# The last stage of a graph network on one core: dinv in all partitions, scaling and transform on GpSimd, ReLU in the residual

## The chip, the cores and the metric

One core of one Trainium2 chip. The metric is the time of one execution on the device, in microseconds (us). The kernel before ran three times: 7513.93 us median, 7498.69 to 7516.11.

## The reference

12500 nodes with 128 features and 412500 edges. Two message-passing layers, each followed by a residual and a layernorm:

```
x = layernorm(x + L0(x))          # filter network on edges, scatter-add, two dense layers
x = layernorm(x + L1(x))

L1: xw = x @ W ;  dinv = rsqrt(degree)
    out = segment_sum(xw[src] * dinv[src] * dinv[dst], dst) + b
    out = (out - mean_over_nodes) * rsqrt(var_over_nodes + 1e-5) * gamma + beta
    return relu(out)
```

The change touches only what comes after the sums of L1: the factor dinv[dst], the batch norm over the nodes, the ReLU, the second residual and the last layernorm.

## The kernel before, in words

`program` runs five parts one after the other, each a block of its own with a program for each engine: `setup`, `filter_layer`, `node_update`, `graph_layer`, `norm_and_store`. The last one is the stage in question. When it begins, `arena` holds the sums of L1 with the 128 features in the partitions and the 12500 nodes along the columns; `x1_tab` in DRAM holds x after the first layernorm; `dinv_tab` in DRAM holds dinv. Nodes are dealt as 125 partitions (NP) times 100 (NC): node p * 100 + c. A batch q is 500 columns (BW); there are 25 batches (NB), each of B = 4 groups of 125 nodes.

Half A runs over the 25 batches. SP loads 500 values of dinv (2 KB) into one partition (L2676); PE multiplies them with a row of ones, so that PSUM holds them in all 128 partitions (L2694, two passes of a float32 matmul for a batch, so 50 in all); DVE multiplies the batch of `arena` in place by that PSUM tile (L2739) and takes its mean and variance with bn_stats (L2742). Two dinv rows and two PSUM tiles are in flight, and the counters `spread` and `scaled` hand them round. Meanwhile ACT's queue has issued five loads of x1 into `xs_flat`, 125 partitions each (L2710). After the last batch, DVE aggregates (L2745) and works out a scale and a shift for each feature in short instructions (L2747 to L2760), with one Sqrt on ACT (L2713).

Half B runs over the 25 batches again, as software pipelines on four engines. ACT waits for `bn_ready`, loads the table with Ln and Exp (L2716), and then in each round:

- transforms a batch: Relu(scale * x + shift), 128x500 (L2722). It reads `rows`, a view of `arena` whose inner step is 100 columns, so 400 bytes, and writes `turned`, dense;
- normalizes the rows of the batch before: four activations of 125x128 (`norm_rows_on_act`, L1842), into one of two `xn` buffers;
- takes the root of the variances as exp(-0.5 * ln(v)) (`norm_root`, L1817 and L1819, 125x4).

PE turns the transformed batch back with four transposes (L2702). DVE adds the PSUM tile to x1 (L2770), takes bn_stats of four rows (`norm_measure`, L1801), aggregates them (L1808), adds the epsilon (L1811, 125x4), and from ACT's root forms the shift of the rows (`norm_shift`, L1834, 125x4). SP stores each batch with one DMA of 125 rows of 2 KB (L2682).

The same helpers run in `node_update`, the part that makes x1. There GpSimd (POOL) is at work too: L1932, L1942 and L1945 are its tensor_tensor instructions of 125x512, and L2134 is a DVE tensor_tensor of 128x500 with both inputs in SBUF. In `setup`, POOL has L462 (affine_select) and L488 (tensor_tensor of 125x256). In `norm_and_store` POOL does nothing before the change.

Of the kernel before, what the change touches and what calls it, by code (L numbers as in the profile page):

```python
# [35 lines left out]
P = 128  # L36
# [13 lines left out]
B = 4  # L50
# [37 lines left out]
WIDE = 112  # L88
X_USED = 5858
MROW = 3 * F + 2  # L90
# [10 lines left out]
def free(g):  # L101
    return g + 1
# [1674 lines left out]
class Norm:  # L1777


    def __init__(self, m, at, sem):  # L1780
# [6 lines left out]
        self.shift = [m.work[0:NP, at + B * (12 + s):at + B * (13 + s)] for s in range(2)]  # L1787
        self.steps, self.waited, self.rooted, self.normed = sem("ln_steps"), sem("ln_waited"), sem("ln_rooted"), sem("ln_normed")
        self.shifted = sem("ln_shifted")
# [32 lines left out]
def norm_rows(nc, dve, m, norm, q, s, out):  # L1822
# [5 lines left out]
    last.then_inc(norm.normed, 1)  # L1828


def norm_shift(nc, dve, norm, q, s):

    dve.wait_ge(norm.rooted, 2 * q + 2)
    nc.vector.scalar_tensor_tensor(norm.shift[s], norm.pair[s][:, :, 0], -1.0, norm.rstd[s], ALU.mult,  # L1834
                                   ALU.mult).then_inc(norm.shifted, 1)


def norm_rows_on_act(nc, act, m, norm, q, s, out):

    act.wait_ge(norm.shifted, q + 1)  # L1840
    for t in range(B):
        last = nc.scalar.activation(out[:, D * t:D * t + D], xs_row(m, q, t), ACT.Identity,  # L1842
                                    bias=norm.shift[s][:, t:t + 1], scale=norm.rstd[s][:, t:t + 1])
    last.then_inc(norm.normed, 1)
# [801 lines left out]
def norm_and_store(nc, m, io):  # L2646

    ps, work = m.ps, m.work
    drow = [work[0:1, 512 * s:512 * s + BW] for s in range(2)]
# [4 lines left out]
    turned = [work[:, 1536 + 512 * s:1536 + 512 * s + BW] for s in range(2)]  # L2654
    xn = [work[0:NP, 2700 + 512 * s:3212 + 512 * s] for s in range(2)]
    ps_d = [ps[:, s, 0:BW] for s in range(2)]
    ps_r = [ps[0:NP, 2 + s, :] for s in range(2)]
    rows = m.arena[:, 0:N].rearrange("f (p c) -> f c p", c=NC)
    with ExitStack() as ctx:
        def sem(name):  # L2660
            return ctx.enter_context(nc.semaphore(name))
        row_in = [sem("dinv_row0"), sem("dinv_row1")]
        spread, scaled, bn_steps, bn_agg = sem("dinv_spread"), sem("sums_scaled"), sem("bn_steps"), sem("bn_aggregated")
        bn_std, bn_ready = sem("bn_std"), sem("bn_ready")
        relu_done, turned_back, res_done = sem("relu_done"), sem("turned_back"), sem("residual2")
        norm = Norm(m, 2600, sem)
        waited = sem("ln2_waited")
        stored = [sem("out_stored0"), sem("out_stored1")]
        x1_in = sem("x1_in")
        block = ctx.enter_context(nc.Block())  # L2670

        @block.sync
        def _(sp):
            def load(q, s, turn):
                sp.wait_ge(spread, free(q))
                sp.dma_start(drow[s], m.dinv_tab[bass.ds(q * BW, BW)].rearrange("(o n) -> o n", o=1)).then_inc(row_in[s], 16)  # L2676
            over(sp, NB, load)
            flat = io["out"].rearrange("(p c) d -> p (c d)", p=NP)

            def store(q, s, turn):  # L2680
                sp.wait_ge(norm.normed, ready(q, 2))
                sp.dma_start(flat[:, bass.ds(q * (B * D), B * D)], xn[s]).then_inc(stored[s], 16)  # L2682
            over(sp, NB, store)
            sp.wait_ge(stored[0], 16 * (NB // 2 + 2))
            sp.wait_ge(stored[1], 16 * (NB // 2 + 1))

        @block.tensor
        def _(pe):
            pe.sem_inc(spread, 2)
# [6 lines left out]
            pe.sem_inc(turned_back, 2)  # L2696

            def back(q, s, turn):
                pe.wait_ge(relu_done, ready(q, 0))
                pe.wait_ge(res_done, free(q))  # L2700
                for t in range(B):
# [105 lines left out]
```

## Time and profile before

| | |
|---|---|
| median of three runs | 7513.93 us |
| profiled execution, its time | 7511.49 us |
| its span, first to last instruction | 7509.8 us |
| mean granted TensorE clock | 0.763 |
| `norm_and_store` in the span | 7339.87 to 7509.8 us |
| half A, first load to the end of the last L2742 | 7339.87 to 7413.39 us |
| half B, from `bn_ready` | 7415.53 to 7509.8 us |

A span is cut into windows to see which engine is busy in which stretch; a row of the timeline is one instruction, or several of a line that follow each other (x4), with its start, its duration, its engine (PE and PEld are TensorE's matmuls and weight loads, DVE is VectorE, ACT is ScalarE, POOL is GpSimd, SP is SyncE), its line, what it writes and reads, and in brackets how long the engine stood idle before it and which instruction ended that. A granted clock of 0.50 is the 1.2 GHz level of TensorE, 1.00 the 2.4 GHz level.

### The profile page before, as it was taken

Reading aid. Unit: us, or ns where it says so; the run is one execution under the profiler, and the core shown is the slowest. Engines: PE = TensorE matmul, PEld = TensorE weight load, DVE = VectorE, ACT = ScalarE, POOL = GpSimd, SP = SyncE. Lnnn points to the kernel's source line nnn. Section 1 sums busy time; section 2 is a strip of 40 time slices with the busy share of each in tenths; the row PEclk is TensorE's granted clock in tenths of the full one; section 3 lists DMA queues with packets and bytes.
Section 4 is the critical chain, followed back from the end, with each engine's and each line's share of the span. In section 5 each row is a group of like instructions: output and inputs, shape, how many; then the busy total and the mean of one; then the engine's idle time right before and its main releaser. Section 6 shows DMA issues by size and latency. Waiting matters only on the chain. (4 is left out here: it accounts for less than half of the span.)

```text
span 7509.8 us, 155131 instructions
## 1 busy us (share of the span) xinstructions
PE 5888.8 (78%) x41800; PEld 4261.6 (57%) x41800; DVE 5381.3 (72%) x14198; ACT 3602.2 (48%) x5657; POOL 5249.8 (70%) x5375
## 2 busy tenths in 40 slices
PE   7777777777777888878777774666999999999994
PEld 6555555555555666666555553554666666666662
DVE  7766767677677888888888884445777777777774
ACT  2555555555555555555555552044333333333334
POOL 4677777777777777777777775534777777777770
PEclk5666666666666667676667776677999999999995
DMA  4222222111113333333333335744222222222222
GB/s 127 79 83 82 84 84 69 55 56 54 55 55 89 111 114 115 110 118 94 93 96 93 93 89 157 248 133 152 77 76 76 77 77 77 76 76 76 76 77 74
DMA packets 512098, 695.12 MB, mean 93 GB/s; under 512 B 255299, under 2 KB 367645, under 8 KB 510879
## 3 DMA queue, kind: packets, MB, share of 16 engines
q1 hardware_dynamic: 317008, 347.69, 16.3%
q0 software_dynamic: 181376, 321.40, 14.5%
q10 hardware_dynamic: 13498, 24.07, 1.0%
q14 instruction: 192, 1.56, 0.1%
q8 instruction: 24, 0.39, 0.0%
HBM read 450.80 MB, written 241.85 MB: 92 GB/s over the span
## 5 line engine op out<-in xcount | busy, mean ns | idle before, releaser
L1688 POOL DMA_INDIRECT msg_tab<-big x3224 | 3318.4, 1029 | 1076.3 <-issue 1076.0
L2239 POOL DMA_INDIRECT big<-y_parts,big x1616 | 1589.2, 983 | 547.7 <-issue 485.5
L2320 ACT CAST big<-ps 128x980 bf16<-128x980 f32 x804 | 783.9, 975 | 1272.3 <-PE ps L2268 1269.6
L2280 PE MATMUL ps<-big 128*128 128x384 bf16 x6566 | 1196.4, 326 | 0.2 <-ACT big L2320 0.2
L2372 DVE TENSOR_SCALAR big<-big,dstF 128x343 bf16<-128x343 f16 (+2 forms) x3216 | 981.9, 338 | 238.5 <-PE ps L2268 235.5
L1187 PEld LDWEIGHTS ps<-big 128*128 128x128 f32 x3224 | 651.4, 300 | 432.9 <-ACT big L1376 432.9
L1187 PE MATMUL ps<-big 128*128 128x128 f32 x3224 | 764.0, 412 | 154.6 <-ACT big L1376 154.6
L1381 ACT CAST big<-big 128x512 bf16<-128x512 f32 x403 | 249.2, 618 | 1213.4 <-DMA msg_tab<-big 1213.0
L1491 DVE TENSOR_TENSOR big<-big 128x512 f32<-128x512 f32 x403 | 279.2, 693 | 762.6 <-ACT big L1381 759.9
L2280 PEld LDWEIGHTS ps<-big 128*128 128x128 bf16 x6566 | 580.5, 97 | 347.9 <-issue 1.0
L1487 DVE TENSOR_REDUCE big<-big 128x8 f32<-128x784 f32 x403 | 637.7, 1582 | 13.7
L1206 PE MATMUL ps<-big 128*128 128x128 f32 x3224 | 632.8, 357 | 0.0
L1206 PEld LDWEIGHTS ps<-big 128*128 128x128 f32 x3224 | 540.9, 254 | 137.6 <-issue 137.6
L1229 PE MATMUL ps<-big 128*128 128x192 bf16 x2037 | 309.8, 324 | 386.4 <-DVE big L1531 386.4
L1197 PEld LDWEIGHTS ps<-big 128*128 128x128 bf16 x9672 | 570.2, 130 | 5.1
L1179 PE MATMUL ps<-big 2*128 2x512 bf16 x806 | 339.0, 512 | 283.0 <-ACT big L1365 283.0
L1197 PE MATMUL ps<-big 128*128 128x64 bf16 x9672 | 554.3, 234 | 0.0
L1229 PEld LDWEIGHTS ps<-big 128*128 128x128 bf16 x2037 | 253.4, 154 | 420.8 <-issue 240.8
L2371 DVE TENSOR_SCALAR big<-big,srcF 128x128 bf16<-128x128 f16 x1608 | 418.8, 260 | 78.3 <-PE ps L2268 72.2
L1369 ACT ACTIVATE big<-big 128x1024 bf16<-128x1024 bf16 x403 | 425.8, 1057 | 63.6 <-ACT big L1365 40.2
L1365 ACT ACTIVATE big<-ps,big 128x1024 bf16<-128x1024 f32 x403 | 441.1, 1095 | 0.0
L2254 PE MATMUL ps<-big 128*128 128x128 bf16 x4848 | 308.6, 221 | 150.8 <-DMA big<-y_parts,big 140.7
(289 smaller groups left out, 10740.7 us busy)
## 6 DMA issues: line engine op xcount, KB each, us to landing
arena<-msg_tab SPq DMA_DIRECT2D x97, 727.5 KB, 4.6
big<-msg_tab SPq DMA_DIRECT2D x97, 630.5 KB, 4.1
big<-in_edge_attr SPq DMA_DIRECT2D x403, 128.0 KB
msg_tab<-big POOLq DMA_INDIRECT x3224
big<-msg_tab SPq DMA_DIRECT2D x97, 388.0 KB, 3.4
msg_tab<-big SPq DMA_DIRECT2D x97, 291.0 KB
big<-y_parts,big POOLq DMA_INDIRECT x1616
big<-h_parts SPq DMA_DIRECT2D x403, 48.0 KB
```

What stands on the lines that cost most here:

```text
L1187: mm = pe.matmul(ps_hid[:, P * q:P * q + P], m.w1_s[:, q % 2, :], attrT[:, P * (q // 2):P * (q // 2) + P], start=True, stop=True)
L1197: mm = pe.matmul(ps_row[:, F * j:F * j + F], pick[s][:, P * j:P * j + P], hwin[s][:, F * n:F * n + F], start=(n == 0), stop=(n == 2))
L1206: mm = pe.matmul(ps_filt[:, P * q:P * q + P], hid[s][:, P * q:P * q + P], m.w2_s[:, :], start=False, stop=(q == J // 2 - 1), skip_group_ch ...
L1229: mm = pe.matmul(ps_seg, hots[:, :, r], seg[s][:, r, 0:3 * F], start=(r == 0), stop=(r == n - 1))
L1365: nc.scalar.activation(far, ps_dst, ACT.Abs, bias=m.negwin[:, bass.ds(g, 1)]).then_inc(far_done, 1)
L1369: nc.scalar.activation(pick[s], far, ACT.Relu, bias=1.0, scale=-1.0, accum_out=count[s]).then_inc(pick_done, 1)
L1487: nc.vector.tensor_reduce(rank[s], prod.rearrange("p h j -> p j h"), AX.X, ALU.add).then_inc(rank_done, 1)
L1688: nc.gpsimd.indirect_dma_start(out=m.msg_tab[:, :], out_offset=bass.IndirectOffsetOnAxis(ap=sidx[s][:, j:j + 1], axis=0), in_=row[s][:, j, ...
L2239: nc.gpsimd.indirect_dma_start(out=m.grow[s][:, 3 * D * j:3 * D * j + 3 * D], out_offset=None, in_=m.y_parts[:, :], in_offset=bass.Indirec ...
L2280: mm = pe.matmul(ps_rows, m.cnt[h][:, a, :], m.y_part[:, HALF * h + a, :], start=(h == 0 and a == 0), stop=(h == 1 and a == HALF - 1))
L2320: nc.scalar.copy(m.cnt[h][:, :, SLOTS * i:SLOTS * i + SLOTS].rearrange("p h (a w) -> p h a w", a=2), ps_cnt[i % 2][:, :, 0:SIDE * HALF].re ...
L2372: last = nc.vector.tensor_scalar(hot_cols(i, t), m.iota_half[:, 0:width_m[t]], 512.0 * h, m.dstF[:, bass.ds(at, 1)], ALU.add, ALU.is_equal)
```

## The change

Half A. SP reads dinv straight from DRAM into all 128 partitions, with six DMAs whose source has a step of 0 over the partitions, into columns of `big` that are free by then (`dinv_bc`); `SPREAD` says which batches each piece covers. Behind them on the same queue it loads x1 in five pieces, each cut in two at partition 112 (`PIECES`), to another place (`x1`). PE does nothing in this half. The scaling multiplies two SBUF operands; batches with q % 5 in (1, 3), ten of 25, are scaled by POOL, the other fifteen by DVE. DVE issues the scaling of batch q + 1 ahead of the bn_stats of batch q. ACT loads the second table right after its Sqrt, without a wait for `bn_ready`.

Half B. The transform of a batch goes from ACT to POOL as a tensor_scalar (multiply, add) without the ReLU; the ReLU goes into the residual, which becomes a scalar_tensor_tensor: max(psum, 0) + x1. DVE's instructions of a round stand in another order: residual(q + 1), offsets(q - 1), pairs(q), measure(q + 1), with_epsilon(q). ACT has only the roots and the rows. Four `xn` buffers in place of two, and each store is cut at partition 112. The loops of the stage are written out in place of hardware loops, so that addresses and counts are constants; each wait on a step of its own stream now has its own semaphore.

```diff
+PIECES = ((0, WIDE), (WIDE, NP))          # WIDE = 112, NP = 125
+XN = 4
+SPREAD = ((0, 2), (2, 5), (5, 10), (10, 15), (15, 20), (20, 25))
+X1_LOADS = 5
...
         @block.sync
         def _(sp):
-            def load(q, s, turn):
-                sp.wait_ge(spread, free(q))
-                sp.dma_start(drow[s], m.dinv_tab[bass.ds(q * BW, BW)].rearrange("(o n) -> o n", o=1)).then_inc(row_in[s], 16)
-            over(sp, NB, load)
+            for k, (a, z) in enumerate(SPREAD):
+                sp.dma_start(dinv_bc[:, a * BW:z * BW],
+                             m.dinv_tab[a * BW:z * BW].rearrange("(o n) -> o n", o=1).to_broadcast([P, (z - a) * BW])
+                             ).then_inc(dinv_in[k], 16)
+            x1_rows = m.x1_tab.rearrange("(p c) d -> p (c d)", p=NP)
+            n = NC * D // X1_LOADS
+            for k in range(X1_LOADS):
+                for a, z in PIECES:
+                    sp.dma_start(x1[a:z, k * n:k * n + n], x1_rows[a:z, k * n:k * n + n]).then_inc(x1_in[k], 16)
...
-            def store(q, s, turn):
-                sp.wait_ge(norm.normed, ready(q, 2))
-                sp.dma_start(flat[:, bass.ds(q * (B * D), B * D)], xn[s]).then_inc(stored[s], 16)
-            over(sp, NB, store)
+            for q in range(NB):
+                sp.wait_ge(normed, q + 1)
+                for a, z in PIECES:
+                    sp.dma_start(flat[a:z, q * (B * D):q * (B * D) + B * D], xn[q % XN][a:z, :]).then_inc(stored[q % XN], 16)
...
+        @block.gpsimd
+        def _(pool):
+            for q in turns:                                   # q % 5 in (1, 3)
+                ...
+                nc.gpsimd.tensor_tensor(part(q), part(q), scales(q), ALU.mult).then_inc(pool_scaled, 1)
+            pool.wait_ge(bn_ready, 4)
+            for q in range(NB):
+                if q > 1:
+                    pool.wait_ge(turned_back, q - 1)
+                nc.gpsimd.tensor_scalar(turned[q % 2].rearrange("f (t p) -> f t p", t=B), rows[:, q * B:q * B + B, :],
+                                        scale, shift, ALU.mult, ALU.add).then_inc(affine_done, 1)
...
         @block.tensor
         def _(pe):
-            def row(q, s, turn):
-                pe.wait_ge(row_in[s], 16 * turn + 16)
-                pe.wait_ge(scaled, free(q))
-                pe.matmul(ps_d[s], m.ones[:, :], drow[s], start=True, stop=True).then_inc(spread, 1)
-            over(pe, NB, row)
+            for q in range(NB):
+                pe.wait_ge(affine_done, q + 1)
+                if q > 1:
+                    pe.wait_ge(res_done, q - 1)
...
         @block.scalar
         def _(act):
             act.wait_ge(bn_agg, 2)
             nc.scalar.activation(std, var_eps, ACT.Sqrt).then_inc(bn_std, 1)
-            act.wait_ge(bn_ready, 4)
             act.preload_act_table_set("natural_log_exp_and_others")
-                    nc.scalar.activation(turned[s].rearrange("f (t p) -> f t p", t=B), rows[:, bass.ds(q * B, B), :],
-                                         ACT.Relu, bias=shift, scale=scale).then_inc(relu_done, 1)
+            root(0)
+            for q in range(NB):
+                norm_rows(q)
+                if q + 1 < NB:
+                    root(q + 1)
...
         @block.vector
         def _(dve):
-                dve.wait_ge(spread, ready(q, 2))
-                nc.vector.tensor_tensor(here, here, ps_d[s], ALU.mult).then_inc(scaled, 1)
+                if not by_pool(q):
+                    nc.vector.tensor_tensor(part(q), part(q), scales(q), ALU.mult).then_inc(scaled, 1)
...
-                nc.vector.tensor_tensor(batch, batch, ps_r[s], ALU.add).then_inc(res_done, 1)
+                nc.vector.scalar_tensor_tensor(batch, ps_r[q % 2], 0.0, batch, ALU.max, ALU.add).then_inc(res_done, 1)
...
+            def with_epsilon(q):
+                dve.wait_ge(paired, q + 1)
+                if q > 1:
+                    dve.wait_ge(normed, q - 1)
+                nc.vector.tensor_scalar(rstd[q % 2], pair[q % 2][:, :, 1], LN_EPS, None, ALU.add).then_inc(with_eps, 1)
+
+            def offsets(q):
+                dve.wait_ge(rooted, 2 * q + 2)
+                nc.vector.scalar_tensor_tensor(offset[q % 2], pair[q % 2][:, :, 0], -1.0, rstd[q % 2], ALU.mult,
+                                               ALU.mult).then_inc(offset_done, 1)
+            for q in range(-1, NB + 1):
+                if q + 1 < NB:
+                    residual(q + 1)
+                if q > 0:
+                    offsets(q - 1)
+                if 0 <= q < NB:
+                    pairs(q)
+                if q + 1 < NB:
+                    measure(q + 1)
+                if 0 <= q < NB:
+                    with_epsilon(q)
```

## Rows read from the trace of the kernel before

**Rows 1.** The core's span; then windows: busy of each engine, PEclk, DMA share, GB/s.

```profile
core 0: 7509.8 us, clock 0.763
...
7370.00:7380.00 10.00, 4.54 (x6) 1.23 (x6) 4.07 (x6) 0.00 (x0) 0.00 (x0) 0.50 0.31 131
...
7390.00:7400.00 10.00, 9.15 (x11) 2.76 (x10) 6.40 (x10) 0.00 (x0) 0.00 (x0) 0.50 0.01 4
...
7440.00:7460.00 20.00, 7.30 (x24) 5.51 (x24) 13.59 (x66) 18.78 (x43) 0.00 (x0) 0.50 0.25 77
```

**Rows 2.** The chain that ended last, two pieces of half A.

```profile
7354.44 4.45 DMA big<-dinv_tab
...
7359.02 2.04 PE ps L2694 x2
```

**Rows 3.** Groups by line of half A: count, busy us, mean ns, idle before.

```profile
L2742 DVE BATCH_NORM_STATS2 big<-arena (+1 forms) x25 | 17.0, 681 | 6.1 <-DVE arena L2739 6.0
L2739 DVE TENSOR_TENSOR arena<-arena,ps 128x500 f32 (+1 forms) x25 | 16.9, 675 | 34.6 <-PE ps L2694 34.0
...
L2694 PE MATMUL ps<-big,ones x50: 1032/1037/1193, 7344.9 to 7410.8; 1*128 1x500 f32 x50
```

**Rows 4.** Timeline of rounds of half B; the last row is from the waits.

```profile
7436.48 1.27 ACT L2722 ACTIVATE big<-arena,big 128x500 f32 x1 [0.23 <-issue]
7436.51 0.69 DVE L2770 TENSOR_TENSOR big<-big,ps 125x512 f32 x1
7437.34 0.87 DVE L1801 BATCH_NORM_STATS2 big<-big 125x6 f32 x4
7437.66 1.63 ACT L1842 ACTIVATE big<-big 125x128 f32 x4
...
7437.81 1.22 PE L2702 MATMUL ps<-ident,big 128*125 128x128 f32 x4 [2.38 <-ACT big L2722]
...
7441.93 0.38 DVE L1808 BATCH_NORM_AGGREGATE big<-big 125x2 f32<-125x6 f32 x4 [0.34 <-DVE big L1801]
7442.35 0.17 DVE L1811 TENSOR_SCALAR big<-big 125x4 f32<-125x4 f32 x1
...
7443.03 0.16 DVE L1834 SCALAR_TENSOR_TENSOR big<-big 125x4 f32<-125x4 f32 x1 [0.51 <-ACT big L1819]
7443.22 1.27 ACT L2722 ACTIVATE big<-arena,big 128x500 f32 x1 [0.23 <-issue]
...
ACT big L1842 <- DMA out<-big: 1.1, 2, 0.7
```

**Rows 5.** A window with 128-row loads; a small load's us to landing (DMA issues).

```profile
5215.00:5220.00 5.00, 0.00 (x0) 0.00 (x0) 4.93 (x6) 0.00 (x0) 4.39 (x3) 0.50 1.11 333
...
big<-agg_parts SPq DMA_DIRECT2D x97, 64.0 KB, 2.9
```

**Rows 6.** Timeline of `node_update`, with POOL and DVE at work together.

```profile
5079.89 0.67 DVE L2134 TENSOR_TENSOR big<-big 128x500 f32<-128x500 f32 x1
5079.97 1.60 POOL L1942 TENSOR_TENSOR big<-big 125x512 f32<-125x512 f32 x1 [3.74 <-ACT big L2071]
...
5092.11 1.16 POOL L1945 TENSOR_TENSOR big<-big 125x512 bf16<-125x512 f32 x1 [0.83 <-ACT big L2077]
5092.33 0.87 DVE L1801 BATCH_NORM_STATS2 big<-big 125x6 f32 x4 [0.15 <-DVE big L2122]
...
5093.23 1.27 POOL L1932 TENSOR_TENSOR big<-big 125x512 f32 x1
...
5093.87 0.65 DVE L1811 TENSOR_SCALAR big<-big 125x4 f32<-125x4 f32 x1
```

**Rows 7.** Single lines, duration in ns min/median/max: POOL in `setup`, ACT's L2057.

```profile
L462 POOL TENSOR_SCALAR_AFFINE_SELECT ident<-ident x1: 284/284/284, 1.4 to 1.4; 128x128 f32<-128x128 f32 x1
...
L2057 ACT ACTIVATE big<-big,half x23: 711/712/715, 4982.5 to 5177.0; 128x500 f32<-128x500 f32 x23
...
L488 POOL TENSOR_TENSOR big<-big,arena x13: 667/1357/3827, 60.4 to 188.1; 125x256 f32<-125x256 f32 x13
```

More of the change, by code:

```diff
@@ L1827, in norm_rows @@
                                        norm.rstd[s][:, t:t + 1], ALU.subtract, ALU.mult)
[L1828 to L1843, printed above, removed]
     last.then_inc(norm.normed, 1)
@@ L2648, in norm_and_store @@
     ps, work = m.ps, m.work
-    drow = [work[0:1, 512 * s:512 * s + BW] for s in range(2)]
+    turned = [work[:, 512 * s:512 * s + BW] for s in range(2)]
     stats = work[:, 1024:1024 + 6 * NB]
@@ L2730, in _, with root, norm_rows @@
-            staged(act, NB, stage)
+            def root(q):
+                act.wait_ge(with_eps, q + 1)
+                nc.scalar.activation(rstd[q % 2], rstd[q % 2], ACT.Ln).then_inc(rooted, 1)
+                act.wait_ge(rooted, 2 * q + 1)
+                nc.scalar.activation(rstd[q % 2], rstd[q % 2], ACT.Exp, scale=-0.5).then_inc(rooted, 1)
+            def norm_rows(q):
+                act.wait_ge(offset_done, q + 1)
+                if q >= XN:
+                    act.wait_ge(stored[q % XN], 32 * (q // XN))
+                for t in range(B):
+                    last = nc.scalar.activation(xn[q % XN][:, D * t:D * t + D], x1_row(q, t), ACT.Identity,
+                                                bias=offset[q % 2][:, t:t + 1], scale=rstd[q % 2][:, t:t + 1])
+                last.then_inc(normed, 1)
@@ L2743, in _, with scale_sums, count_sums @@
-            over(dve, NB, scale_sums)
+            def scale_sums(q):
+                for k, (a, z) in enumerate(SPREAD):
+                    if q == a:
+                        dve.wait_ge(dinv_in[k], 16)
+                if not by_pool(q):
+                    nc.vector.tensor_tensor(part(q), part(q), scales(q), ALU.mult).then_inc(scaled, 1)
+            def count_sums(q):
+                if by_pool(q):
+                    dve.wait_ge(pool_scaled, turns.index(q) + 1)
+                else:
+                    dve.wait_ge(scaled, q + 1 - len([k for k in turns if k < q]))
+                nc.vector.bn_stats(stats[:, q * 6:q * 6 + 6], part(q)).then_inc(bn_steps, 1)
@@ L2744, in _ @@
+            scale_sums(0)
+            for q in range(NB):
+                if q + 1 < NB:
+                    scale_sums(q + 1)
+                count_sums(q)
             dve.wait_ge(bn_steps, NB)
@@ L2774, in stage, with residual @@
-            def stage(before, here, after):
-                if before:
-                    norm_shift(nc, dve, norm, *before[:2])
-                if here:
-                    residual(*here)
-            staged(dve, NB, stage)
+            def residual(q):
+                for k in range(X1_LOADS):
+                    if q == -(-k * NB // X1_LOADS):
+                        dve.wait_ge(x1_in[k], 32)
+                dve.wait_ge(turned_back, q + 1)
+                batch = x1[:, q * (B * D):q * (B * D) + B * D]
+                nc.vector.scalar_tensor_tensor(batch, ps_r[q % 2], 0.0, batch, ALU.max, ALU.add).then_inc(res_done, 1)
@@ new lines, in measure, with pairs @@
+            def measure(q):
+                dve.wait_ge(res_done, q + 1)
+                for t in range(B):
+                    last = nc.vector.bn_stats(row_stats[q % 2][:, t, :], x1_row(q, t))
+                last.then_inc(measured, 1)
+            def pairs(q):
+                dve.wait_ge(measured, q + 1)
+                for t in range(B):
+                    last = nc.vector.bn_aggr(pair[q % 2][:, t, :], row_stats[q % 2][:, t, :])
+                last.then_inc(paired, 1)
+            def with_epsilon(q):
[3 more added lines that the diff above has]
+                nc.vector.tensor_scalar(rstd[q % 2], pair[q % 2][:, :, 1], LN_EPS, None, ALU.add).then_inc(with_eps, 1)
```

83 lines of the change are left out of this document (32 added, 51 removed).

## The prediction

> **What bounds the kernel now.** I read the per-core line first, then the windows of the end of the span. The profiled execution has a span of 7509.8 us [rows 1] and a time of 7511.49 us; the median of the runs is 7513.93 us, 2.4 us more. The diff touches only `norm_and_store`, which runs from 7339.87 to 7509.8 us: 170 us, 2.3% of the whole. It has two halves with different limits, and the windows show them: in the first the DMA engines are busy at 0.31 and then idle, in the second ACT is busy 18.78 of 20 us [rows 1].
>
> First half, A, 7339.87 to 7413.39 us (end of the last L2742): 73.5 us. The chain of work alternates a landing of `dinv_tab` (4.5 us for 2 KB) and two or four passes of L2694 [rows 2]. The rows of dinv land slowly while the five loads of x1 (6.4 MB) run at 131 GB/s with a DMA share of 0.31, which is 5 of 16 engines [rows 1]. From 7391 us that share is 0.01, and the reader should see what takes over: PE, two passes of 1.037 us for a batch at the granted clock of 0.5. DVE has 16.9 us in L2739 and 17.0 us in L2742, so it is idle for over half of the 73.5 us [rows 3].
>
> Second half, B, from the last small DVE instruction (7415.53 us) to the end, 7509.8 us: 94.3 us. A table load of 1.28 us, then 25 rounds of 3.37 us (L2722 starts at 7436.48 and, two rounds on, at 7443.22). In a round ACT has the transform L2722 (1.27), L1842 (1.63 for its four) and Ln and Exp (0.20 each): 3.3 us, no idle time but issue. DVE has 0.69 + 0.87 + 0.38 + 0.17 + 0.16 = 2.27 us, PE 1.22 us, POOL nothing [rows 4]. The chain of waits ran through the stores of 3.96 us, but ACT waited for them for only 1.1 us in all [rows 4]: ACT's work is what repeats.
>
> **The change, part by part: half A.** Removed: 25 small loads and 50 matmuls. Added: one read of dinv into 128 partitions (6.4 MB, six pieces) and x1 behind it on the same SP queue, cut at partition 112. A load with 128 rows moved 333 GB/s at a DMA share of 1.11, one with 125 rows 131 GB/s at 0.31 [rows 1, 5]. At 333 GB/s dinv takes 19 us and x1 another 19. The Trainium skill ("DMA: Bandwidth & Descriptors", why a DMA increments its semaphore by 16) says that the row count decides over how many engines a load is spread, the largest divisor up to 16: 5 for 125 rows and 16 for 128 or 112; the share of 0.31 agrees.
>
> No load that reads one DRAM row into all partitions stands in the trace. Its bounds are the two rates: 6.4 MB in 19 us or in 49 us. I take the fast one, since the destination is 128 rows as in the fast row. The first piece (0.5 MB) needs 2.9 us, the landing of a small load with nothing beside it [rows 5], plus 1.5: 4.4 us. After it pieces arrive faster than DVE uses them (3.9 us for five batches).
>
> DVE: 15 scalings and 25 bn_stats. A scaling with both inputs in SBUF took 0.68 us for 128x500 [rows 6], bn_stats 0.68 [rows 3]; with a gap of 0.05 that is 40 x 0.73 = 29.3 us. POOL: ten scalings, 1.16 us each for 125x512 [rows 6], 12 to 13 us with gaps, beside DVE. They are not free of each other. When DVE's L2134 began at 5079.89, L1942 on POOL began 0.08 later and lasted 1.60 instead of 1.16 us: it stood until L2134 was done. In the other direction L1811, 0.17 us alone, lasted 0.65 and ended at 5094.52, when POOL's L1932 ended (5093.23 + 1.27 = 5094.50) [rows 6]. So DVE's scaling and POOL's exclude each other, while bn_stats (0.87 for four with POOL at work and without [rows 4, 6]) does not care. Each of the ten POOL scalings then holds a DVE scaling for what bn_stats does not cover, 1.16 - 0.68 = 0.5 us: 5 us. Half A: 4.4 + 29.3 + 5 = 38.7 us, a gain of 34.8. Bounds: 33.7 (no exclusion) to 58 (dinv at the slow rate: 2.9 + 48.9 for the last piece, and its five batches 6).
>
> x1's first piece lands at 4.4 + 18 + 4, before half A ends; cover, so no cost. The second table load no longer waits for `bn_ready` and goes behind the Sqrt while DVE computes five small instructions (0.9 us of its 1.28; the rest is before ACT's first root): its 1.28 leave the path.
>
> **Half B, a round.** ACT loses L2722: 1.63 + 0.41 + two handovers, about 2.4 us. DVE keeps its 2.27 and gets the ReLU inside an instruction of the same length (L2770, 0.69). In the new order its round is residual .69, offsets .16, pairs .38, measure .87, epsilon .17 with five gaps of 0.05: 2.5 us. Ln and Exp (0.51 us from DVE's side [rows 4]) now lie under the next residual. Without anything else a round would take 2.5 us.
>
> POOL gets the transform: 128x500, one input, read with a stride of 400 bytes. The trace of before has none. Below: POOL's one-input AFFINE_SELECT took 0.284 us for 128 columns [rows 7]; with 0.1 of it taken as fixed (an estimate), the rest is 1.43 ns a column, and 500 columns are 0.1 + 0.72 = 0.82 us. Above: the two-input 1.16 us times what the stride costs ACT (L2722 1.27 against L2057 0.71, both 128x500 from SBUF [rows 4, 7]): 2.1 us. I take 1.3, the middle in ratio.
>
> When does it run? POOL's batch q+4 waits for the transposes of q+2, which wait for the residual of q. From the end of a residual: 1.22 us of transposes, 0.2 to start POOL (an estimate: the gaps before other engines' released instructions are 0.02 to 0.1, and between L1942 and L1945 POOL stood idle 0.83 around an ACT instruction of 0.62 [rows 6]): POOL starts at 1.45. DVE comes to epsilon at 0.05 + .16 + .05 + .38 + .05 + .87 + .05 = 1.6. So POOL has begun 0.15 us before the instruction of the form of L1811, the one that rows 6 show held until POOL is done. It ends at 1.45 + 1.3 + 0.02, then gap and residual 0.74: a round of 3.5 us, 2.2 plus POOL's instruction. ACT (2.4) and the roots (0.51 under the residual's 0.74) stay hidden.
>
> The Trainium skill ("SBUF — State Buffer", Who interferes with whom) has this as an exclusive lock of a port pair that VectorE and GpSimd share, taken by a tensor_scalar in a two-port mode and by an instruction with two SBUF inputs; rows 6 agree for both, and by it `offsets` (two SBUF inputs) could be held too, but not the residual, whose second input is PSUM. Without this rule the sum for B would be that of rounds of 2.5 us, 24 us less.
>
> The Trainium skill ("GPSIMD Engine Reference", Performance pitfalls) gives POOL 2.9 cycles an element for a step over 8 bytes: an estimate of 1.2 us for 500 elements at its 1.2 GHz, and by it a round of 3.4.
>
> Ends of B: first transform 1.5, transposes 1.27, residual 0.8: 3.6 us. From the last residual: epsilon done at 1.75, roots 0.5, offsets, pairs and epsilon of the last batch 1.0, then ACT's rows of the batch before (till 4.1), roots 0.5, offset 0.2, rows 1.65, store 3.1: 9.8 us. The store is 3.96 less 1.2 (256 KB at 333 instead of 131 GB/s) plus 0.3 for the second issue. Four buffers and pieces change the rounds by nothing: ACT waited 1.1 us for stores in all. SP's queue issues two stores of 0.3 us a round. B: 3.6 + 24 x 3.5 + 9.8 = 97.4 us, 3.1 more than 94.3.
>
> **Sum.** 7511.5 - 34.8 + 3.1 = 7479.8; against the median, 2.4 higher: 7482 us. So I expect the gain in half A, and a half B that has turned a 3.4 us round set by ACT into one set by DVE waiting for POOL.
>
> **Rivals.** (1) No collision: epsilon gets in before POOL, or POOL's start slides. The margin is 0.15 us, made of gaps that I read from a loop that disappears. Round 2.5, B = 73.4, time 7513.9 - 34.8 - 20.9 = 7458. Collisions in every second round would give 3.0 and 7470. (2) The read of dinv runs at the 131 GB/s: A is 58 us, 7513.9 - 15.5 + 3.1 = 7501. For it: 16 engines read one and the same 10 KB. Against it: no row. (3) POOL's transform at its upper bound, 2.1 us: round 4.3, B = 116.6, 7501. (4) The other side: POOL is far slower with the stride. L488, 125x256, took 0.667 us at best and 3.827 at worst [rows 7]; at 3.8 us a round is 6.0, B = 157.4, and the time 7542. It decides from 2.6 us on, where B's loss equals A's gain; over 3.6 the kernel is slower by more than 0.3%. Against it: the long L488 are the ones held by others, the short one repeats.
>
> **How the numbers follow.** Forecast 50%, rival 1 20%, rival 2 13%, rival 3 11%, rival 4 6%. 0.3% is 22.5 us, about what a measurement of this kernel can tell from no change (its three runs lie 17 us apart). Below 7491 are the forecast (but for a twelfth: a round over 3.9) and rival 1: 0.46 + 0.20, and some of rivals 2 and 3, whose bounds are less than full: 0.72 in all. Slower by 0.3% is rival 4 above 3.6 us: 0.05. The range holds rival 1 to rivals 2 and 3: 7455 to 7503.
>
> **What would show it.** Right: A near 39 us with PE idle; POOL's transform 1.3 us, DVE's `with_epsilon` lasting about 1.2 us instead of 0.17 and ending with POOL; 3.5 us from residual to residual; ACT idle a third of B. Wrong: `with_epsilon` at 0.17 and rounds of 2.5 (rival 1); DVE waiting for `dinv_tab` in A (2); a POOL instruction above 2 us (3, 4); or `offsets` held instead of `with_epsilon`, which would mean that POOL starts later than I worked out.

## The result and the profile after

The changed kernel takes 7413.14 us (median of four runs, 7401.91 to 7423.92), the kernel before 7506.31 us in the same comparison (median of four, 7484.49 to 7516.11): a ratio of 0.9886, 95% interval 0.987 to 0.9903. The gain is 93 us where 32 were forecast, and the time lies 42 us below the lower end of the range. The prediction was wrong. The kernel is faster, as forecast, but the forecast had only half A gaining, and half B gained as well. The 42 us are not the difference between executions either: the stage alone, 72 us shorter (below), would give 7442 us from the median that the prediction started from, still below the range.

The profiled execution has a span of 7400.2 us, 109.6 us less than before. First I asked how much of that lies in the stage that was changed. It now starts at 7302.3 us (first load of dinv) and takes 97.9 us instead of 169.9: 72.0 us less. The other 37.6 us lie ahead of it, in code that the diff does not touch. The halves, cut as in the prediction (2.1 us of small instructions lie between them):

| | half A | half B | a round of B |
|---|---|---|---|
| before | 73.5 us | 94.3 us | 3.37 us |
| forecast | 38.7 | 97.4 | 3.5 |
| after | 30.5 | 65.3 | 2.21 |

Windows of the changed kernel, two of half A and one of half B. The columns are PE, PEld, DVE, ACT and POOL, then the granted clock, the DMA share and GB/s, as in [rows 1]:

```profile
7310.00:7315.00 5.00, 0.00 (x0) 0.00 (x0) 4.56 (x9) 0.00 (x0) 3.27 (x3) 0.50 0.99 422
7325.00:7330.00 5.00, 0.00 (x0) 0.00 (x0) 5.00 (x10) 0.00 (x0) 1.28 (x1) 0.50 0.91 229
7345.00:7385.00 40.00, 21.48 (x75) 16.66 (x74) 34.07 (x202) 35.18 (x109) 22.31 (x18) 0.50 0.43 130
```

Half A has no PE work, DVE is idle only where it waits for dinv's second and third piece (0.67 and 0.44 us) once it runs, and the DMA share is 0.99 where it was 0.31 and 0.01. Dinv arrives at 422 GB/s and x1 behind it at 229. Half B is still closest to ACT (35.18 of 40 us), as it was before, but in rounds of two thirds of the length.

The groups of half A, by line (compare [rows 3]), and a few of its instructions from the timeline:

```profile
L2703 POOL TENSOR_TENSOR arena<-arena,big 128x500 f32<-128x500 f32 x10 | 17.2, 1747 | 12.4 <-DMA big<-dinv_tab 12.4
L2761 DVE BATCH_NORM_STATS2 big<-arena 128x6 f32<-128x500 f32 x25 | 15.9, 666 | 0.0
L2754 DVE TENSOR_TENSOR arena<-arena,big 128x500 f32<-128x500 f32 x15 | 10.9, 723 | 6.9 <-DMA big<-dinv_tab 6.9
```

```profile
7306.95 0.68 DVE L2754 TENSOR_TENSOR arena<-arena,big 128x500 f32<-128x500 f32 x1 [5.75 <-DMA big<-dinv_tab]
7307.00 1.73 POOL L2703 TENSOR_TENSOR arena<-arena,big 128x500 f32<-128x500 f32 x1 [10.33 <-DMA big<-dinv_tab]
...
7316.58 0.68 DVE L2761 BATCH_NORM_STATS2 big<-arena 128x6 f32<-128x500 f32 x1
7317.17 1.12 DVE L2754 TENSOR_TENSOR arena<-arena,big 128x500 f32<-128x500 f32 x1
```

The scaling (L2754 on DVE, L2703 on POOL) is the exclusion of [rows 6] again, but the loser is mostly POOL: all ten of its scalings meet one of DVE's and take 1.67 to 1.79 us, 1.75 on average, instead of the 1.16 of [rows 6], while DVE was held in only two of fifteen (1.12 instead of 0.66). The last two rows show something else that matters for the whole: L2761 begins at 7316.58 and lasts 0.68, so it ends at 7317.26, and the next instruction has begun at 7317.17. DVE's instructions are 0.59 us apart, not 0.68 plus a gap.

A round of half B in the timeline (compare [rows 4]):

```profile
7347.11 1.65 ACT L2738 ACTIVATE big<-big 125x128 f32<-125x128 f32 x4 [0.23 <-DVE big L2813]
7347.28 0.84 DVE L2796 BATCH_NORM_STATS2 big<-big 125x6 f32<-125x128 f32 x4
...
7348.12 0.68 DVE L2791 SCALAR_TENSOR_TENSOR big<-ps,big 125x512 f32<-125x512 f32 x1
7348.66 0.19 ACT L2729 ACTIVATE big<-big 125x4 f32<-125x4 f32 x1
7348.88 0.21 ACT L2731 ACTIVATE big<-big 125x4 f32<-125x4 f32 x1
...
7348.95 1.19 PE L2718 MATMUL ps<-ident,big 128*125 128x128 f32 x4 [1.03 <-DVE big L2791]
7349.12 0.16 DVE L2813 SCALAR_TENSOR_TENSOR big<-big 125x4 f32<-125x4 f32 x1 [0.32 <-ACT big L2731]
...
7349.49 0.84 DVE L2796 BATCH_NORM_STATS2 big<-big 125x6 f32<-125x128 f32 x4
7350.24 1.26 POOL L2708 TENSOR_SCALAR big<-arena,big 128x500 f32<-128x500 f32 x1 [0.99 <-PE ps L2718]
7350.24 0.15 DVE L2809 TENSOR_SCALAR big<-big 125x4 f32<-125x4 f32 x1
7350.31 0.69 DVE L2791 SCALAR_TENSOR_TENSOR big<-ps,big 125x512 f32<-125x512 f32 x1
```

The residual (L2791) begins at 7348.12 and again at 7350.31: 2.19 us, and L2813 2.21 us after its last one. The epsilon (L2809) begins in the same hundredth as POOL's transform and takes 0.15 us. The forecast collision is missing from the steady rounds. It happens once, at the first epsilon of the half, while POOL still runs ahead of its later rhythm: that epsilon begins 0.55 us after a transform of POOL (7340.22 us) and takes 0.69 us. The second one begins 0.13 us after POOL's and is free:

```profile
7340.77 0.69 DVE L2809 TENSOR_SCALAR big<-big 125x4 f32<-125x4 f32 x1
...
7343.49 1.23 POOL L2708 TENSOR_SCALAR big<-arena,big 128x500 f32<-128x500 f32 x1 [0.85 <-PE ps L2718]
...
7343.62 0.15 DVE L2809 TENSOR_SCALAR big<-big 125x4 f32<-125x4 f32 x1
```

The chain of work that ended last, in the same stretch, names what sets the round instead: ACT's four rows, its two roots, and one offset on DVE.

```profile
7346.91 0.17 DVE big L2813
...
7347.11 1.65 ACT big L2738 x4
...
7348.88 0.21 ACT big L2731
...
7349.12 0.17 DVE big L2813
```

### The profile page after: what moved, and what is told of

The parts are those of the page before. It is cut to its first block and busy times, and to the rows that moved or that the text cites. A ratio compares the mean times of both kernels' runs of the same rounds, so it can differ in the third digit from the quotient of the medians.

```text
span 7400.2 us, 154124 instructions
## 1 busy us (share of the span) xinstructions
PE 5795.9 (78%) x41750; PEld 4211.8 (57%) x41750; DVE 5361.6 (72%) x14188; ACT 3573.3 (48%) x5632; POOL 5260.4 (71%) x5410
## 5 line engine op out<-in xcount | busy, mean ns | idle before, releaser
L1192 PEld LDWEIGHTS ps<-big 128*128 128x128 f32 x3224 | 639.0, 295 | 429.3 <-ACT big L1381 429.3
L1192 PE MATMUL ps<-big 128*128 128x128 f32 x3224 | 749.5, 405 | 152.2 <-ACT big L1381 152.2
L2267 PEld LDWEIGHTS ps<-big 128*128 128x128 bf16 x6566 | 580.5, 97 | 347.9 <-issue 1.2
L1211 PE MATMUL ps<-big 128*128 128x128 f32 x3224 | 626.8, 355 | 0.0
L1211 PEld LDWEIGHTS ps<-big 128*128 128x128 f32 x3224 | 535.4, 252 | 136.4 <-issue 136.4
L1202 PEld LDWEIGHTS ps<-big 128*128 128x128 bf16 x9672 | 560.5, 129 | 4.9
L1234 PEld LDWEIGHTS ps<-big 128*128 128x128 bf16 x2037 | 247.2, 153 | 442.7 <-issue 226.8
```

The source lines that it names most:

```text
L1192: mm = pe.matmul(ps_hid[:, P * q:P * q + P], m.w1_s[:, q % 2, :], attrT[:, P * (q // 2):P * (q // 2) + P], start=True, stop=True)
L1202: mm = pe.matmul(ps_row[:, F * j:F * j + F], pick[s][:, P * j:P * j + P], hwin[s][:, F * n:F * n + F], start=(n == 0), stop=(n == 2))
L1211: mm = pe.matmul(ps_filt[:, P * q:P * q + P], hid[s][:, P * q:P * q + P], m.w2_s[:, :], start=False, stop=(q == J // 2 - 1), skip_group_ch ...
L1234: mm = pe.matmul(ps_seg, hots[:, :, r], seg[s][:, r, 0:3 * F], start=(r == 0), stop=(r == n - 1))
L2267: mm = pe.matmul(ps_rows, m.cnt[h][:, a, :], m.y_part[:, HALF * h + a, :], start=(h == 0 and a == 0), stop=(h == 1 and a == HALF - 1))
```

## The experiments

One table for all of them: the halves from the trace, the stage (A + 2.1 + B), and the ratio to the kernel before. The column "stage alone" is 1 less the stage's gain over 169.9 us, divided by 7506.

| kernel | A | B | stage | stage alone | ratio, 95% interval |
|---|---|---|---|---|---|
| changed | 30.5 | 65.3 | 97.9 | 0.9904 | 0.9886 (0.987 to 0.9903) |
| after_again | 30.3 | 65.2 | 97.7 | 0.9904 | 0.9898 (0.9875 to 0.992) |
| half_a_alone | 30.4 | 105.2 | 137.7 | 0.9957 | 0.9953 (0.9938 to 0.9969) |
| half_b_alone | 73.8 | 65.3 | 141.3 | 0.9962 | 0.9958 (0.9943 to 0.9974) |
| epsilon_late | 30.3 | 73.1 | 105.5 | 0.9914 | 0.9912 (0.9891 to 0.9933) |
| filler_behind_epsilon | 30.4 | 66.6 | 99.1 | 0.9906 | 0.9907 (0.9892 to 0.9922) |
| dve_scales_all | 34.2 | 65.3 | 101.6 | 0.9909 | 0.9905 (0.989 to 0.992) |
| act_transforms | 30.5 | 134.4 | 167.0 | 0.9996 | 0.9998 (0.9988 to 1.0008) |
| act_transforms_early | 30.3 | 124.1 | 156.5 | 0.9982 | 0.9981 (0.9972 to 0.9991) |
| act_transforms_far | 30.4 | 88.7 | 121.3 | 0.9935 | 0.9933 (0.9917 to 0.995) |
| dve_old_order | 30.4 | 87.3 | 119.9 | 0.9933 | 0.994 (0.9923 to 0.9957) |
| two_buffers | 30.5 | 71.6 | 104.3 | 0.9913 | 0.9915 (0.9898 to 0.9931) |
| one_piece_stores | 30.3 | 70.0 | 102.5 | 0.9910 | 0.9906 (0.9889 to 0.9922) |
| two_buffers_one_piece | 30.4 | 85.3 | 117.9 | 0.9931 | 0.9931 (0.9914 to 0.9947) |
| roots_a_batch_ahead | 31.6 | 57.6 | 91.3 | 0.9895 | 0.9894 (0.9876 to 0.9912) |

**The change a second time.** No edit. 

> The changed kernel once more, unchanged, in five rounds. In the first traces its last stage is 97.9 us long instead of 169.9, so 72 us shorter, but it also starts 37.6 us earlier, in stages whose code is the same. Theory (the stage is all of it; the 37.6 us are how executions differ in the clock granted to the matmuls of the long stages): the ratio is 0.9904 (7506 - 72), within 0.001, the stage again 98 us, and the start of the stage anywhere within some 20 us of 7330. Rival (the change also shortens earlier stages, for instance by the length or place of the program): the stage starts near 7302 again and the ratio is 0.9855 to 0.988.

The stage starts at 7315.2 us in this trace instead of 7302.3, and takes 97.7 us. Over all traces of a kernel whose earlier code is the same, its start lies between 7302.3 and 7343.7 us (before: 7339.87). So the 37.6 us ahead of the stage are what one execution differs from another, and only the 72 us are the change. The table says the same: in every row "stage alone" is within 0.0007 of the ratio, except for the changed kernel's first comparison, where it is 0.0018 off and just outside the interval.

**Each half alone.** half_a_alone is the kernel before with the new half A; half_b_alone is the changed kernel with the old half A:

```diff
 half_a_alone: half A as changed, half B as before, with one wait for all of x1
+            dve.wait_ge(x1_in, 160)
 half_b_alone: the loads, the pass of ones and the scaling of half A as before,
               x1 by five loads of 125 rows on ACT's queue
+                act.dma_start(x1[:, k * n:k * n + n], x1_rows[:, k * n:k * n + n]).then_inc(x1_in[k], 32)
```

> The kernel before with only half A changed (dinv read into all partitions, POOL scales ten batches, x1 behind it in two pieces); half B has its loops, roles and stores as before. If the gains of the halves are separate, A is 30.5 us as in the changed kernel instead of 73.5, half B stays at 94.3, and the kernel gains 43 us: ratio 0.9943. Rival (x1, which now lands later, or its new place costs half B something): B over 96.

> The changed kernel with half A as before (rows of dinv through PE and PSUM, all scaling on DVE, x1 in 125-row loads on ACT's queue). If the gains are separate: A 73.5 us, B 65 us in rounds of 2.21, and a gain of 29 us: ratio 0.9961. Rival (x1 and dinv had to be fast for B to be fast): rounds above 2.3.

Measured: gains of 32.2 and 28.6 us, rounds of 3.37 and 2.21. So half B is the larger part of my miss: forecast at a loss of 3.1, it gains 29. The two gains make 60.8 us, and both edits together make 72.0. The missing 11 stand in one row of half_a_alone's timeline:

```profile
7383.79 0.69 DVE L2795 TENSOR_TENSOR big<-big,ps 125x512 f32<-125x512 f32 x1 [15.11 <-DMA big<-x_tab]
```

The old half B waits once for all of x1, which now goes behind dinv and lands 47.6 us after the stage's start. In the kernel before the same instruction stood 4.0 us idle, for PE's transposes, so this costs 11.1 us. The changed kernel waits for x1 piece by piece and never notices. I had written of x1's first piece that it lands in time; it is the wait by pieces that makes this enough.

**Does the collision exist?** Two kernels with one more DVE instruction a round, a bn_stats of 125x128 (0.27 us) into unused columns: ahead of the epsilon, so that it comes after POOL has begun, and behind it as the control.

```diff
 epsilon_late
+                if 0 <= q < NB - 1:
+                    nc.vector.bn_stats(work[0:NP, 1300:1306], x1_row(q + 1, 0)).then_inc(filled, 1)
                 if 0 <= q < NB:
                     with_epsilon(q)
 filler_behind_epsilon: the same two lines behind with_epsilon(q)
```

> The changed kernel with one more bn_stats of 125x128 (0.2 us, its result is used by nothing) ahead of with_epsilon in each round. Theory (DVE's epsilon and POOL's transform exclude each other, and in the changed kernel epsilon gets in first by less than 0.1 us): epsilon now starts 0.2 us behind POOL, lasts about 1.1 us instead of 0.16 and ends with POOL's instruction, and the round goes from 2.21 to about 2.9 to 3.2 us, B 16 to 24 us longer. Rival (the collision is harmless, or POOL is what waits): epsilon stays at 0.16 and the round at 2.21 to 2.3, since DVE has 0.34 us of slack in a round.

> The control to the run with the late epsilon: the same extra bn_stats (0.2 us, used by nothing) stands behind with_epsilon. Theory (only epsilon's place beside POOL's start matters): DVE's slack of 0.34 us takes it up, the round stays at 2.21, epsilon at 0.16 us. Rival (the extra work as such lengthens the round): 2.4.

The control costs 1.3 us over the changed kernel, the filler ahead of the epsilon 7.8 us. The timeline of epsilon_late:

```profile
7387.77 0.15 DVE L2810 TENSOR_SCALAR big<-big 125x4 f32<-125x4 f32 x1
...
7387.97 1.22 POOL L2709 TENSOR_SCALAR big<-arena,big 128x500 f32<-128x500 f32 x1 [2.05 <-PE ps L2719]
...
7388.66 0.54 DVE L2814 SCALAR_TENSOR_TENSOR big<-big 125x4 f32<-125x4 f32 x1
...
7389.95 1.22 POOL L2709 TENSOR_SCALAR big<-arena,big 128x500 f32<-128x500 f32 x1 [0.76 <-PE ps L2719]
...
7390.36 0.83 DVE L2810 TENSOR_SCALAR big<-big 125x4 f32<-125x4 f32 x1
```

The epsilon that comes 0.41 us after POOL's start takes 0.83 us and ends at 7391.19, within 0.02 us of POOL's end (7389.95 + 1.22). So the mechanism that I forecast is real, at this distance; the Trainium skill ("SBUF — State Buffer", Who interferes with whom) has it as a lock of a shared port pair, and this agrees, also in that an instruction with two SBUF inputs (L2814, 0.54 instead of 0.16) can be held. But it costs a third of what I expected of this kernel: a held epsilon delays the next residual and with it POOL's next start, so the next epsilon (here at 7387.77, ahead of POOL at 7387.97) is free. Two rounds take 5.25 us instead of 4.42 or the 7.0 of my forecast.

How far behind POOL's start an epsilon is still free can be read from the traces of all kernels. The latest free ones begin 0.13 to 0.16 us after it, one in each of seven traces (the changed kernel's is shown above), and take 0.14 to 0.15 us. The earliest held one begins 0.23 us after it and takes 1.02 (7416.24 us in two_buffers_one_piece); in the same trace an offset that begins 0.19 us after it takes 1.03. So for the epsilon the border lies between 0.16 and 0.23 us, and the 0.15 us by which I had POOL ahead would not have been enough.

**Half A without POOL.**

```diff
-        return q % 5 in (1, 3)
+        return False
```

> The changed kernel with all 25 scalings on DVE, none on POOL. In the changed kernel DVE works without a pause in half A at 0.585 us from one instruction to the next, and two of its scalings were held for 0.46 us by POOL. Theory (DVE is the limit, POOL's share takes ten of its instructions away): A is longer by 10 x 0.585 - 0.9 = 4.9 us, 35.4 instead of 30.5. Rival (the exclusion eats what POOL takes over): A within 1.5 us of 30.5.

Half A is 34.2 us instead of 30.5, 3.7 more (4.9 expected). Ten more instructions of 0.59 us are 5.9. Nearly all of the difference of 2.2 us can be read from the two traces: the two held scalings are 0.9; the changed kernel's DVE, which needs dinv sooner, waits 0.65 us longer for its later pieces (1.12 against 0.47); and its first scaling starts 4.63 us after the first load instead of 4.19, before POOL has done any work in the stage. The same half A takes 30.3 to 30.5 us in all traces but one, where it takes 31.5.

**The transform back on ACT.** POOL's loop is removed; ACT has `transform(q)`, an Identity activation with the same scale and shift, at three distances:

```diff
 act_transforms
+            transform(q + 2)
             norm_rows(q)
             root(q + 1)
 act_transforms_early
             norm_rows(q)
+            transform(q + 3)
             root(q + 1)
 act_transforms_far: transform(q + 4) in the place of early's
```

> The changed kernel with the transform of half B back on ACT (same function without the ReLU, 1.27 us; ReLU stays in the residual). Theory (a round is ACT's chain: rows 1.65, Ln and Exp, offset, and the transform is what POOL takes off it): the round is 2.21 + 1.27 = 3.5 us less what fits into ACT's wait for the offset (0.23), so 3.25 to 3.5, and B about 26 to 31 us longer, near that of the kernel before. Rival (the written-out loops and the new order of DVE give most of B's gain): a round of 2.6 or less.

> The transform back on ACT as in act_transforms, but issued one round earlier (batch q + 3 behind the rows of q). In the first try a round was 5.2 us, because DVE's order puts residual(q + 2) ahead of offsets(q), and ACT made the transform for that residual just before it waited for that offset: a chain of 1.25 + 1.22 + 0.69 + 0.15 + 1.65 + 0.4. Theory (that chain was mine, and ACT's own work is the limit otherwise): a round is 1.65 + 1.25 + 0.41 + 0.1, so 3.35 to 3.5 us, B 27 to 30 us longer than 65.3. Rival (without POOL, whatever the order, the transform's way over ACT costs more): 4 us or more.

> The transform on ACT once more, now for batch q + 4 behind the rows of q. With q + 3 the round was still 4.9 us: offsets(q + 1) stands behind residual(q + 3) in DVE's order, and that residual needs the transform made just before, so the chain 1.25 + 1.22 + 0.69 + 0.15 + 1.65 was still closed. Theory: with q + 4 it is open, ACT's own work is the limit, a round is 1.65 + 1.25 + 0.41 + 0.1 = 3.4 us, half B 94 us (65.3 + 24 x 1.2). Rival: the round stays above 4.

The first took 5.24 us a round and the second 4.9, where ACT's own work is 3.3. Both expectations missed it. The timeline of act_transforms_early gives the reason:

```profile
7415.44 1.25 ACT L2724 ACTIVATE big<-arena,big 128x500 f32<-128x500 f32 x1
...
7416.74 1.22 PE L2712 MATMUL ps<-ident,big 128*125 128x128 f32 x4 [3.69 <-ACT big L2724]
...
7418.00 0.69 DVE L2797 SCALAR_TENSOR_TENSOR big<-ps,big 125x512 f32<-125x512 f32 x1 [3.03 <-PE ps L2712]
7418.60 0.15 DVE L2819 SCALAR_TENSOR_TENSOR big<-big 125x4 f32<-125x4 f32 x1
...
7418.79 0.88 ACT L2738 ACTIVATE big<-big 125x128 f32<-125x128 f32 x2 [1.77 <-DVE big L2819]
```

In DVE's new order the offsets of batch q stand behind the residual of batch q + 2. The residual waits for the transform, the rows wait for the offsets, and the next transform stands behind the rows: a ring of 1.25 + 1.22 + 0.69 + 0.15 + 1.65 = 4.96 us, where no engine is full. With the transform four batches ahead the ring opens, and the round is 3.37 us, as in the kernel before (B is 5.6 us shorter than there, mostly by its first three rounds, of 1.5 to 1.8 us):

```profile
7394.03 0.16 DVE L2819 SCALAR_TENSOR_TENSOR big<-big 125x4 f32<-125x4 f32 x1 [1.49 <-ACT big L2731]
...
7394.23 1.65 ACT L2738 ACTIVATE big<-big 125x128 f32<-125x128 f32 x4 [0.23 <-DVE big L2819]
...
7395.78 1.25 ACT L2724 ACTIVATE big<-arena,big 128x500 f32<-128x500 f32 x1
```

**DVE's order as before.** The transform stays on POOL.

```diff
             for q in range(NB + 1):
                 if q > 0:
                     offsets(q - 1)
                 if q < NB:
                     residual(q); measure(q); pairs(q); with_epsilon(q)
```

> The changed kernel with DVE's order of before: offsets(q - 1), then residual, measure, pairs and epsilon of one batch, each waiting for the one ahead of it. Everything else is the changed kernel. Theory (half of B's gain is this order: no instruction waits for the one just ahead of it, and the root lies under the next residual): a round is 0.16 + 0.69 + 0.15 + 0.87 + 0.26 + 0.38 + 0.17 and 0.51 for the root, about 3.2 us, so B 24 us longer, as before the change, though ACT has lost its 1.27 us. Rival (the transform on POOL is what gives the gain): a round under 2.6.

3.26 us a round, B 87.3. Here POOL does hold DVE, in the offsets:

```profile
7396.12 1.21 POOL L2708 TENSOR_SCALAR big<-arena,big 128x500 f32<-128x500 f32 x1 [2.05 <-PE ps L2718]
...
7396.72 0.63 DVE L2813 SCALAR_TENSOR_TENSOR big<-big 125x4 f32<-125x4 f32 x1 [0.51 <-ACT big L2731]
7397.27 0.68 DVE L2791 SCALAR_TENSOR_TENSOR big<-ps,big 125x512 f32<-125x512 f32 x1
```

0.51 us of waiting for the roots and 0.47 of waiting for POOL (0.63 instead of 0.16) stand in the open. So in a steady round moving ACT's transform to POOL gains 0.11 us without DVE's new order, and the new order gains nothing without the move; with their other rounds the two kernels shorten B by 7.0 and 5.6 us, where both together give 29. The loops are written out in both, so that alone does not give the gain either.

**The stores.** Two buffers instead of four, one store of 125 rows instead of two pieces, and both.

```diff
 two_buffers
-XN = 4
+XN = 2
 one_piece_stores
-                for a, z in PIECES:
+                for a, z in ((0, NP),):
```

> The changed kernel with two xn buffers instead of four, stores still in two pieces. ACT may write a buffer again when the store of two batches before has landed. At rounds of 2.21 it has 2 x 2.21 - 1.65 = 2.77 us for that. If a store in two pieces lands in about 3.1 us as I forecast: two rounds take 1.65 + 3.1 + 0.2, a round 2.5, B 6 us longer. Rival (it lands within 2.7): no change.

> The changed kernel with each store as one DMA of 125 rows, four buffers. A store of the kernel before landed in 3.96 us; with four buffers ACT has 4 x 2.21 - 1.65 = 7.2 us. Theory (only the landing time counts): the round stays at 2.21 us, and only the last store is longer, 1 to 1.3 us. Rival (125 rows on 5 engines cannot carry 256 KB in 2.21 us): at 131 GB/s a store moves in 1.95 us, so it should just fit; if not, the round is over 2.3.

> Both undone: two buffers and one DMA of 125 rows per store, as before the change. Theory: two rounds take 1.65 + 3.96 + 0.2 us for the way to SP and back, a round 2.9, B about 17 us longer, with ACT waiting for the DMA. So buffers and pieces, which I had priced at nothing, are worth that only because the rest of the round is short, and each alone nearly suffices. Rival: they change nothing.

Each costs little alone (6.3 and 4.8 us), both together 20.0. With two buffers in pieces most rounds stay at 2.21, and ACT waits four times. The longest wait, 4.3 us, is for the very first store (issued at 7372.6 us), while the DMA engines are still busy with x1 (share 0.93 from 7370 to 7375 us), so most of the 6.3 us is paid once and not in every round. With both undone ACT waits 21 times. The waits for a store, first of two_buffers, then of two_buffers_one_piece (us, count, longest):

```profile
ACT big L2738 <- DMA out<-big: 7.0, 4, 4.3
```

```profile
ACT big L2738 <- DMA out<-big: 22.4, 21, 4.3
```

In one_piece_stores the price is at the end. A window of it, after the last residual:

```profile
7415.00:7420.00 5.00, 0.00 (x0) 0.00 (x0) 1.41 (x11) 4.48 (x15) 0.00 (x0) 0.50 0.32 107
```

256 KB in 2.21 us are 116 GB/s, and the stores of 125 rows move 107 to 128 from 7375 us on, at a DMA share of 0.32 to 0.34, 5 of 16 engines. That is what the rounds ask, with nothing to spare, and the first stores were late already: they ran beside the last of x1 (share 0.96 from 7360 to 7370 us). The share stays at 0.32 to the end, so the delay is never made up. The last rows are ready at 7420.62 us and the span ends at 7428.1, 7.5 us later; in the changed kernel it is 2.7 us.

**A version that follows from this.** The chain of the changed kernel passes roots, offset and rows in series. Here the roots of q + 1 go ahead of the rows of q on ACT, the offsets to the end of DVE's loop, and the three small tiles get four buffers:

```diff
             for q in range(NB):
+                if q + 1 < NB:
+                    root(q + 1)
                 norm_rows(q)
-                if q + 1 < NB:
-                    root(q + 1)
...
-                if q > 1:
-                    dve.wait_ge(normed, q - 1)
+                if q > 3:
+                    dve.wait_ge(normed, q - 3)
```

> The changed kernel with ACT taking the root of batch q + 1 before the rows of batch q, offsets last in DVE's order, and four instead of two buffers for pairs, roots and offsets. Theory (the round is the loop rows, epsilon to root, offset, rows, in which ACT stands for about 0.25 us for the offset): ACT no longer stands, the round is 1.65 + 0.41 + two gaps, 2.05 to 2.1 us, B 3 to 4 us shorter. Rival (epsilon or offsets now meet POOL's instruction): a round over 2.3.

> The same kernel as roots_a_batch_ahead, one look. There half B was 57.6 us instead of 65.3, twice the 3 to 4 us that I had expected, with DVE without a pause in 1.78 us and ACT in 1.87. If that is the kernel and not the execution, B is within 1 us of 57.6 again, wherever in the span the stage starts.

B is 57.6 us and, in the second kernel run, 57.5: 7.7 us less than the changed kernel, where 3 to 4 were expected. A window of the second run:

```profile
7380.00:7400.00 20.00, 13.16 (x45) 10.22 (x46) 20.00 (x123) 19.68 (x65) 13.73 (x12) 0.50 0.47 141
```

DVE is busy 20.00 of 20 us, in rounds of 1.78 us from residual to residual. In the whole time this is 0.1%: the ratio of 0.9894 can't be told from the changed kernel's 0.9886 and 0.9898. It beats it by the traces' stage (91.3 and 90.0 us against 97.9 and 97.7), not by the medians.

## Why the prediction was wrong

- **The step that failed** is "DVE comes to epsilon at 0.05 + .16 + .05 + .38 + .05 + .87 + .05 = 1.6. So POOL has begun 0.15 us before". POOL's side was right: it starts 1.44 us after the end of a residual (7348.80 to 7350.24; 1.45 forecast) and its transform takes 1.23 us (1.3 forecast). DVE's side was not. I put a gap of 0.05 us between its instructions; an instruction that waits for nothing new begins 0.07 to 0.09 us before the recorded end of the one ahead. So DVE too comes to the epsilon at 1.44 us, although it first stood 0.32 us for ACT's root, which I had not forecast at that place. It gets in, and the round has no wait for POOL. The second half of the step failed too: POOL 0.15 us ahead does not hold the epsilon. It is free up to 0.16 us behind POOL's start in seven traces and held from 0.23 us on, so with DVE's 1.6 us the forecast would still have had no wait. The forecast took "POOL has begun" for enough, from a row where POOL had begun 0.64 us before (L1932 and L1811 of [rows 6]). A gap of 0.04 like those that I went by stands in [rows 4], between L1808 and L1811 of the old loop; the overlap stood in `node_update` of the kernel before, in the instruction that follows the first one of [rows 6]:

```profile
5080.48 1.04 DVE L2138 COPY arena<-ps 128x500 f32 x1
```

  L2134 would end at 5080.56 by its duration, and the next instruction begins at 5080.48, as it does after a long instruction all through the changed kernel.

- **Rival 1 was the right mechanism**, by the margin that I had named, though the margin was counted wrong. Its size was off: DVE's round was put at 2.5 us, and DVE's own work is 1.78 (measured where DVE is the limit, in roots_a_batch_ahead). What sets the changed kernel's 2.21 us is ACT: rows 1.65, Ln and Exp, and the offset with its handovers. I had put ACT's loop at 2.4 and called it hidden.
- **The collision itself** was right as a mechanism and wrong as a cost: it is not paid in every round, since it delays its own cause. In epsilon_late a round takes 2.6 us on average, filler included, not 3.5.
- **Half A**: 30.5 us instead of 38.7. The first scaling starts 4.6 us after the first load (4.4 forecast). 40 instructions at 0.585 us are 23.4 instead of 29.2 (written as 29.3 in the prediction; 5.8 us of the miss, the same wrong gap). The exclusion took 0.9 us instead of 5: I had DVE as the loser every time, and it was POOL. Another 1.1 us went for dinv's second and third piece, for which I had no wait.
- **Dinv's read**: fast, as taken; 406 to 438 GB/s instead of 333. Rival 2 is out, and so are 3 and 4: POOL's transform is 1.23 us, and act_transforms_far shows what the move is worth. x1 came more slowly than taken, at 225 to 240 GB/s instead of 333, and in the changed kernel nothing waited for it.
- **Stores**: "Four buffers and pieces change the rounds by nothing" was argued from waits of 1.1 us in rounds of 3.37 us. It held for the rounds that I forecast, not for those of 2.21. Undone together they cost 20.0 us.
- **Ends of half B**: 3.4 us at the start (3.6 forecast), 9.3 at the end (9.8, though the terms written there add up to 9.55).
- The table load behind the Sqrt (1.28 us) is hidden, as forecast.

Sum of the miss in the stage: 8.2 us in A and 32.1 in B (of which 24 x 1.3 = 31 in the rounds), 40.3 of the 61 us between the forecast and the measured gain; the rest is the difference between executions ahead of the stage.

What stays open: why the one that begins first can be the one held. In five of the ten scalings of half A POOL's began 0.03 to 0.04 us ahead of DVE's and was held, and no epsilon up to 0.16 us behind POOL's start was. These runs show the distances, not the cause. The clock of the stages ahead of this one was not followed either, so why executions differ there by up to 41 us is open.

## What to carry to other kernels

Before a collision of two engines is put at a margin of 0.15 us, take the distance from start to start of instructions that follow each other, not durations plus a gap: here four gaps of the wrong sign turned a free round into a forecast wait. And take from the traces how far apart the two starts were where one was held: 0.64 us there says nothing about 0.15. When a round is near several limits at once (here, with any one of them put back: ACT's work 3.37 us, DVE's order 3.26, the stores 2.85), lifting one shows little, lifting all shows 1.2 us a round, and the part that looks idle in the old profile is the one to recount at the new speed. A wait by pieces is part of the gain of loading later: with one wait for the whole, half_a_alone lost 11 of the 43 us that its half A gained.

## What the runs showed of the hardware

- A load that repeats one DRAM row into 128 partitions moved 406 to 438 GB/s, by the count of the windows, where the load of different rows in [rows 5] moved 333. The x1 pieces of 112 and 13 rows moved 225 to 240.
- Between POOL's and DVE's tensor_tensor from SBUF, whichever began second was not always the one held: in half A all ten of POOL's took 1.67 to 1.79 us instead of 1.16, five of them though they had begun 0.03 to 0.04 us first. DVE's took 1.12 instead of 0.66 in two, which began 1.2 us after POOL's.
- The small epsilon instruction was not held when POOL's had begun up to 0.16 us before (0.15 us, two_buffers); it was when POOL's had begun 0.23 us before (1.02 us, two_buffers_one_piece) or 0.41 us before (0.83 us, epsilon_late).
- A DVE instruction that waited for nothing new began 0.07 to 0.09 us before the recorded end of the one ahead: 0.585 us from start to start for 0.66 us recorded (128x500).
- POOL's tensor_scalar of 128x500 with an input step of 400 bytes took 1.23 us, ACT's activation over the same input 1.25.
